# A graph and mixture-of-experts kernel on one core: expert weights in another column order, with one table of first biases

## The reference

```python
gate_logits = x @ gate_w + gate_b
topk_vals, topk_idx = jax.lax.top_k(gate_logits, K)
topk_w = jax.nn.softmax(topk_vals, axis=-1)
h = jax.nn.relu(jnp.einsum('bsh,ehf->bsef', x, w1) + b1)
expert_out = jnp.einsum('bsef,efh->bseh', h, w2) + b2
sel = jnp.take_along_axis(expert_out, topk_idx[:, :, :, None], axis=2)
moe = jnp.sum(topk_w[..., None] * sel, axis=2)
```

## Time and profile before

| | |
|---|---|
| median of 3 runs | 2982.95 us |
| profiled execution, span from first to last instruction | 2982.4 us |
| first product of the expert stage starts | 2511.13 us |
| last output of the stage is added | 2874.70 us |
| tiles in the stage | 64 |
| TensorE busy over the span | 2197.4 us, 74% |
| DMA queue of SP, share of 16 engines' span | 16.1% |

### The profile page before, as it was taken

The page is one execution under the profiler, slowest core; times in us unless marked ns, Lnnn a source line. Parts: engine busy times, 40 slices in busy tenths (PEclk is TensorE's granted clock), DMA queues, the critical chain, the costliest instruction groups (busy, mean ns, idle before and its releaser), DMA issues.

```text
span 2982.4 us, 45692 instructions
## 1 busy us (share of the span) xinstructions
PE 2197.4 (74%) x11212; PEld 1870.1 (63%) x11212; DVE 1652.5 (55%) x3901; ACT 1065.1 (36%) x2376; POOL 1349.8 (45%) x1214
## 2 busy tenths in 40 slices
PE   2338788887878888787888877888886613999950
PEld 1226676776667777666677756666675603999950
DVE  3547766665766666677666667766664530000016
ACT  1125444443543444354344344434432311222210
POOL 3144555555555555555555655555562045000035
PEclk9659899998989999898999989889997756999985
DMA  6632222223222222322222232222222115777743
GB/s 191 200 97 52 63 59 58 60 61 101 53 67 56 58 59 63 97 56 66 57 59 59 64 90 60 57 55 58 55 66 64 51 44 155 253 253 255 257 138 101
DMA packets 275286, 281.07 MB, mean 94 GB/s; under 512 B 149948, under 2 KB 216344, under 8 KB 275120
## 3 DMA queue, kind: packets, MB, share of 16 engines
q0 software_dynamic: 128000, 130.89, 17.9%
q1 hardware_dynamic: 147120, 148.50, 16.1%
HBM read 238.22 MB, written 39.96 MB: 93 GB/s over the span
## 4 chain that ended last, share of the span: by engine, by line
PE 42%; issue 17%; DVE 14%; DMA 8%; ACT 7%; POOL 6%; SPq 3%; DVEq 3%; POOLq 0%; ACTq 0%
PE bank L1044 20%; PE bank L1253 8%; DMA G<-P_d,stage 5%; ACT TT L812 4%; PE bank L1261 4%; DVE z L402 3%; POOL G L423 3%; PE bank L1038 3%; POOL slot_in L749 2%; PE bank L1098 2%; PE bank L354 1%; PE bank L362 1%; PE bank L355 1%; DVE hn L1383 1%; DMA aT<-attr_d 1%
## 5 line engine op out<-in xcount | busy, mean ns | idle before, releaser
L423 POOL DMA_INDIRECT G<-P_d,stage x896 | 1164.2, 1299 | 946.5 <-DVE z L402 669.4
L370 ACT ACTIVATE zr<-z 125x512 fp32r<-125x512 f32 x448 | 276.2, 635 | 719.3 <-DVE z L402 534.1
L402 DVE TENSOR_TENSOR z<-bank,G 125x512 f32<-125x512 f32 x448 | 295.6, 686 | 364.9 <-DMA G<-P_d,stage 208.1
L1044 PE MATMUL bank<-W_s,hid 128*125 128x256 f32 x1600 | 363.6, 382 | 0.0
L1044 PEld LDWEIGHTS bank<-W_s,hid 128*125 128x125 f32 x1600 | 295.8, 190 | 44.0
L354 PE MATMUL bank<-zr,onehot 125*125 125x256 f32 x896 | 282.7, 344 | 15.2 <-DVE zl L376 13.7
L1038 PE MATMUL bank<-ident,hn 125*128 125x125 f32 x700 | 144.5, 317 | 200.5 <-DVE hn L1383 87.8
L376 DVE SCALAR_TENSOR_TENSOR zl<-z,zr 125x512 fp32r<-125x512 f32 x448 | 287.4, 682 | 2.0 <-ACT zr L370 0.2
L1177 PE MATMUL bank<-TTh,W_h 128*128 128x250 f32 (+1 forms) x640 | 219.2, 342 | 77.5 <-ACT hid L907 54.3
L1038 PEld LDWEIGHTS bank<-ident,hn 125*128 125x128 f32 x700 | 81.3, 153 | 258.7 <-ACT TT L812 53.4
L355 PE MATMUL bank<-zl,onehot 125*125 125x256 f32 x896 | 240.6, 296 | 0.0
(11 more groups left out here) (283 smaller groups left out, 3938.5 us busy)
## 6 DMA issues: line engine op xcount, KB each, us to landing
W_s<-in_L_ffn_w SPq DMA_DIRECT2D x64, 512.0 KB, 3.9
hid<-in_L_ffn_w SPq DMA_DIRECT2D x64, 512.0 KB, 3.9
G<-P_d,stage POOLq DMA_INDIRECT x896
slot_in<-yo SPq DMA_DIRECT2D x8, 1024.0 KB, 10.3
W_s<-in_L_mix_W SPq DMA_DIRECT2D x8, 1024.0 KB, 10.6
aT<-attr_d SPq DMA_DIRECT2D x224, 31.2 KB
xs<-slot_in SPq DMA_DIRECT2D x32, 128.0 KB, 2.1
b2e<-in_L_ffn_b SPq DMA_DIRECT2D x32, 128.0 KB, 4.2
```

Of the source, the lines that this page charges most:

```text
L370: nc.scalar.activation(zr[:, s, k, :], z[:, k, :], ACT.Relu).then_inc(r_done, 1)
L402: nc.vector.tensor_tensor(z[:, k, :], edge_bank[k][0:ET, :], G[:, ST * s + 2 * k:ST * s + 2 * k + 2, :].rearrange("p j d -> p (j d)"), ALU ...
L423: nc.gpsimd.indirect_dma_start(G[:, j, :], None, P_d[:, :], bass.IndirectOffsetOnAxis(ap=stage[s][:, j:j + 1], axis=0)).then_inc(g_in[j], 16)
L1044: ins = pe.matmul(to[0:parts, 0:cols], a, b, start=i == 0, stop=i == len(products) - 1)
```

## The change

W1 chunks are read with a step of two columns. Hidden unit f = 256 h + 2 p + j stands on partition p, with chunk number c = 2 h + j: chunk c takes the columns from 256 (c // 2) + c % 2 with step 2, 8 bytes. W2's rows for one partition are then 2 x 2 rows, so its load has 256 pieces of 2 KB in place of 128 pieces of 4 KB. The first bias has pieces of 8 bytes in HBM; all 16 experts' biases are therefore loaded once, at the program's start, into a new table `b1_all` (128 x 64) by a DMA that ACT issues, and each tile's `b1e` is copied from it, SBUF to SBUF, by the DMA that stood there for the load from HBM. SP waits for the table once, before the first tile.

```diff
         b1e = [sb(f"b1e{i}", [128, NFE]) for i in range(XB)]
+        b1_all = sb("b1_all", [128, NE * NFE])
...
-                load(b1e[s][:, :], eb1[ds(ex, 1), :].rearrange("o (p c) -> p (o c)", c=NFE), w1_in[s])
-                load(W2e[s], ew2[ds(ex, 1)].rearrange("o (p c) d -> p (o c) d", c=NFE), w2_in[s])
+                load(b1e[s][:, :], b1_all[:, ds(ex * NFE, NFE)], w1_in[s])
+                load(W2e[s].rearrange("p (h j) d -> p h (j d)", j=2), ew2[ds(ex, 1)].rearrange("o (h p j) d -> p (o h) (j d)", p=128, j=2), w2_in[s])
                 load(b2e[s], eb2[ds(ex, 1), :].to_broadcast([128, D]), w2_in[s])
             sp.wait_ge(r_pos, 3)
+            sp.wait_ge(b1_in, 16)
...
+            with nc.allow_non_contiguous_dma(reason="short vectors to columns"):
+                act.dma_start(b1_all[:, :].rearrange("p (h j) -> p h j", j=2), eb1.rearrange("e (h p j) -> p (e h) j", p=128, j=2)).then_inc(b1_in, 16)
...
-                        ins = pe.matmul(RING[1 + s % 2][:, c * SL:(c + 1) * SL], W1e[s][:, k, c::NFE], xT[s % 2][:, k, :],
+                        ins = pe.matmul(RING[1 + s % 2][:, c * SL:(c + 1) * SL], W1e[s][:, k, c // 2 * 256 + c % 2:c // 2 * 256 + 256:2], xT[s % 2][:, k, :],
                                         start=k == 0, stop=k == KD - 1)
```

More of the change, by code:

```diff
@@ L270, in build @@
         gw_in, par_in, dst_in, br_in, late_in = sem("gw_in"), sem("par_in"), sem("dst_in"), sem("br_in"), sem("late_in")
+        b1_in = sem("b1_in")
         consts, cdep, wparts_done, ws_done, wT_T, wT_cp = (sem(n) for n in ("consts", "cdep", "wparts_done", "ws_done", "wT_T", "wT_cp"))
```

## The result

The changed kernel takes 2918.81 us (median of 4, 2907.56 to 2922.41), the kernel before 2982.93: a ratio of 0.9769, 95% interval 0.9744 to 0.9794. That is 64 us less, inside the range of 2870 to 2932, but 29 us short of the 2890 forecast.

The account below looks back on a forecast made before the run. TensorE was taken to bound the expert stage at 5.68 us a tile, DMA next. Savings of 87.3 (period), 5.7 (first tiles) and 2.0 (last `up`), less 2.3 (table), gave 92.7: 2982.95 to 2890 us, range 2870 to 2932.

Parts of the forecast that it names:

- The step of W1's columns: Weight loads of `up`: 8-byte step costs 0.11 us each instead of 0.232, so `up` takes 1.76 us instead of 3.71.
- B: Rival on `up`'s weight loads: 8-byte step costs as much as 16, total 2983 to 2987 us; chance 0.09.
- C: Rival on TensorE's clock: idle time drops it to 1.2 GHz, 7.4 us a tile, total 3084 us; chance 0.04.
- The period of 4.2: Expert stage's steady part: a tile takes 4.2 us instead of 5.68, saving 87.3 us over 59 periods.
- loop through `xs`: Slots issued after tile m - 4's output, landing in 2.1 us: 7.4 us for two periods, 3.7 each.
- SP's 3.96: SP's queue in the expert stage: issuing six transfers and reading the expert's number takes 3.96 us a tile, a floor.
- My own forecast: Main case for the expert stage: period of 3.96 to 4.5 us, ending at 2908 us at the slow end; chance 0.67.
- rival A: Expert stage: DMA feeds only 302 GB/s, period 4.8, or the 8-byte step is half free; total 2928 us, chance 0.2.
- What I weighed for DMA: DMA engines in the expert stage: 3.80 us a tile at 381 GB/s, 4.79 at 302; 4.43 us current occupation.
- sign of about 345 GB/s: Expected in the steady part of the profile after: DMA share above 0.9 and about 345 GB/s.
- The first tiles: Start of the expert stage: `up` of tile 1 saves about 1.7 us, tiles 2 and 3 save 2 each, together 5.7.
- The table's load: Program start, ACT's queue: 4096 pieces of 8 bytes cost 2.3 us, with bounds 0 and 10.

Follow-up runs that it names:

- change_again: The changed kernel itself, run once more beside other variants: 2917.42 us, ratio 0.9764 to the kernel before.
- tables_direct: The changed kernel without per-tile loads of either bias; ACT and DVE read both from tables at an address from a register: 2893.34 us, ratio 0.9677.
- half_w2: The changed kernel, but each tile loads only half of W2, in 256 pieces of 1 KB: 2912.61 us, ratio 0.9741.
- stride_alone: The kernel before with only the 8-byte step of W1's columns; W2 and first bias loaded as before: 2908.79 us, ratio 0.9727.
- b1_pieces: The changed kernel without the table; each tile loads its first bias from HBM in 256 pieces of 8 bytes: 2918.59 us, ratio 0.9747.
- no_b1_issue: The changed kernel without the per-tile copy of the first bias; ACT reads expert 0's from the table: 2907.58 us, ratio 0.9703.
- loads_alone: The changed kernel with the 16-byte step of W1's columns kept: 2983.87 us, ratio 0.9986.
- step3: The kernel before with a step of 3 columns (12 bytes) in W1's stationary operand, nothing else changed: one run of 2935.57 us.

## Why the prediction was right, and where it was not

**The step of W1's columns.** Right. I took 0.11 and it is 0.117; B is out. The rule that I weighed against the rows (SBUF — State Buffer in the Trainium skill, the note on "cachelines") is borne out: two hits in a 16-byte line are nearly enough (0.117 against 0.108). `up` lost 1.83 us of the 1.95 forecast. The clock kept 1.00 in the steady part of this profile, so C is not what happened. In change_again it did happen, to two tiles of that stretch, after TensorE had stood idle for 2.97 and 3.21 us. Their `up`, and the clock of the first:

```profile
2620.86 3.21 PEld L1258 LDWEIGHTS bank<-xT,W_s 128*128 128x128 f32 x16
2636.64 3.00 PEld L1258 LDWEIGHTS bank<-xT,hid 128*128 128x128 f32 x16
2620.80:2624.00 3.20, 3.20 (x18) 3.20 (x18) 0.00 (x0) 0.39 (x1) 0.00 (x0) 0.56 1.02 360
```

Over the whole stretch the clock was still 0.98.

**The period of 4.2.** This is the term that was mis-sized: 59 x (5.68 - 4.2) = 87.3 us. In the profiled execution `up` of tile 4 starts at 2520.50 and of the last at 2790.31, 4.57 a tile (before: 5.67), so it gave 65 us. Two of its inputs were off.

The loop through `xs` was worked out with the landing time of before, 2.1 us, and I said myself that each microsecond behind older transfers adds a half, but put that at nothing. With the change the slots are issued while W2 and the second bias of the tile before still flow, and land in 3.5. By the same sum: 1.17 + 3.5 + 0.33 + 1.88 + 1.64 + 0.4 = 8.9 us for two periods, 4.46. For tables_direct, with 3.0, it gives 4.2 against 4.30 measured, and for half_w2, with 3.3, 4.36 against 4.52. It is thus some 0.1 short, and where that goes is open. So is which of the older transfers the slots wait for: halving W2 took only 0.2 us off their landing. Early slots took this wait away and nothing else, and the period fell to 4.38.

SP's 3.96 was taken over unchanged ("the same issue on SP"), but a copy from SBUF is issued for 0.50 us, not 0.33, and the load behind it for 0.54, not 0.38. Its floor is 4.3. In the changed kernel this is nearly hidden behind the slots (stride_alone, b1_pieces, no_b1_issue), and it is the bound when the slots are early: 4.38 against 3.87 without the bias's issue. Either one alone gives little: 4.51 with SP relieved, 4.38 with early slots; both together give 3.87.

**The range** held by luck. My own forecast, a period of 3.96 to 4.5 with a chance of 0.67, ended at 2908 us (2910 with the table's 2.3, which I left out there). The measured 4.57 and 2918.81 lie beyond it. They are within the range only because rival A's 2928 was let in, and neither half of A came true: the step is not half free, and the engines can feed 371 GB/s.

**What I weighed for DMA** was right in kind: 4.43 us of occupation was not a capacity. The fed rate of 381 GB/s from 6 us of trace proved nearer (371 over 170 us) than the 302 of the first burst. But rival A's 4.8, which rests on the 302, and my 4.2 both look at the wrong resource. The sign of about 345 GB/s was off too: 319, with the engines shown as full.

**The first tiles** gave 1.7 us, not 5.7: after `up` of tile 3 and `down` of tile 2 TensorE waited for tile 4's slots, and then ran at half clock. The timeline of weight loads, the wait as the products show it, and the clock of the `up` behind it:

```profile
2514.69 1.60 PEld L1266 LDWEIGHTS bank<-hid,QT 128*128 128x128 f32 x8
2520.23 0.29 PEld L1251 LDWEIGHTS bank<-ident,xs 128*128 128x128 f32 x2 [3.94 <-issue]
2520.50 3.54 PEld L1258 LDWEIGHTS bank<-xT,W_s 128*128 128x128 f32 x16
2790.31 2.06 PEld L1258 LDWEIGHTS bank<-xT,hid 128*128 128x128 f32 x16
2520.26 0.66 PE L1251 MATMUL bank<-ident,xs 128*128 128x128 f32 x2 [3.57 <-DMA xs<-slot_in]
2520.50:2524.10 3.60, 3.60 (x18) 3.60 (x18) 0.00 (x0) 0.38 (x1) 0.00 (x0) 0.50 1.00 324
```

`up` takes 3.54 us there, 0.21 a record, where it takes 1.96 at full clock: what the halved clock costs is now more than what the step costs. With early slots this pause is gone.

**The table's load** was forecast at 2.3 us on the engines. From 0 to 12 us of the profile after:

```profile
q10 hardware_dynamic: 4079, 0.03, 19.7%
b_all<-in_L_ffn_b ACTq DMA_DIRECT2D x1, 32.0 KB, 12.3
```

19.7% of 12 us is 2.4 us of each engine. Whether any of it reaches the end is open: loads_alone, which has it, is within its interval of no change.

**The whole.** From the first `up` to the last the stage took 289.6 us in place of 356.3: 65 of the 59 periods and 1.7 of the first tiles, 67 less. The last `up` adds 1.7. That is 68 in place of the 95 forecast before the table was taken off, and the period makes 22 of the difference. The profiled execution is 77 us shorter. It reached the stage 10 us earlier than the one before did. The other profiles of kernels that are equal up to there reach it between 9 us before and 18 us after 2511 us, so this part is scatter of the earlier stages. The medians' 64 us agree with the stage's 68 within that scatter and what the table may take.

## What to carry to other kernels

In this kernel the load of a float32 stationary operand of 128 columns cost 0.117 us with a step of 8 bytes and 0.232 with 16, by the 16-byte pieces of a row that it touches. So choose the order of a free index so that neighbouring columns share a line, if need be by loading the other operands in the same order. When a bound engine is made faster, redo the sum of every loop that feeds it with the latencies of the fuller queue, not with those of before, and load first what is wanted first. A DMA share near 1 doesn't show that the engines are the limit: here it stood beside 319, 329, 340 and 371 GB/s, and twice TensorE was the bound. Look at the issuing queue and its order before cutting bytes.

## What the runs showed of the hardware

Sixteen loads with a step of 16 bytes take 3.83 us at clock 0.50 and 3.81 at 1.00; with 8 bytes it is 3.54 and 1.96. With 12 bytes (step3) it is 3.54 and 2.88: at half clock the 12-byte step costs nothing over the 8-byte one. The clock of the first `up` in the kernel before, then step3's first `up` and its clock:

```profile
2510.90:2514.80 3.90, 3.90 (x18) 3.85 (x17) 0.00 (x0) 0.38 (x1) 0.62 (x1) 0.50 1.01 338
2512.66 3.54 PEld L1253 LDWEIGHTS bank<-xT,W_s 128*128 128x128 f32 x16
2512.70:2516.00 3.30, 3.30 (x17) 3.30 (x16) 0.00 (x0) 0.39 (x1) 0.63 (x1) 0.50 1.02 330
```

The DMA engines are shown as occupied for 0.97 of the time at 319 GB/s (the change) and for 1.02 at 371 GB/s with the slots issued a tile earlier and without the 2 KB copy. An issue of 2 KB from SBUF at an address from a register held SP for 0.50 us, and the next one for 0.54; with the same 2 KB from HBM (b1_pieces) it was 0.38 and 0.42.
